# First stage of a two-layer perceiver kernel: queries and values moved between the key chunks, ones rows filled later, maxima over 96 rows

## What is computed

```python
def _L0_xattn_ref(queries, keys, values, Wq, bq, Wk, bk, Wv, bv, Wo, bo):
    q = (queries @ Wq + bq).reshape(B, L, 16, 8).transpose(0, 2, 1, 3)
    k = (keys @ Wk + bk).reshape(B, S, 16, 8).transpose(0, 2, 1, 3)
    v = (values @ Wv + bv).reshape(B, S, 16, 8).transpose(0, 2, 1, 3)
    weights = jax.nn.softmax(jnp.einsum('bhld,bhsd->bhls', q, k) * SCALE, axis=-1)
    out = jnp.einsum('bhls,bhsd->bhld', weights, v).transpose(0, 2, 1, 3).reshape(B, L, 128)
    return out @ Wo + bo

x = x + _L0_xattn_ref(_layernorm(x), ctx, ctx, ...)
x = x + _L0_attn_ref(_layernorm(x), ...)
x = x + _L0_ffn_ref(_layernorm(x), ...)
# and the same three again for layer 1, whose cross attention normalises queries and keys by head
```

## Time and profile before

| | us |
|---|---|
| median of 3 runs (362.95 to 363.93) | 363.71 |
| span of the profiled execution | 361.7 |
| PE busy | 317.0 (88%) |
| DVE busy | 229.4 (63%) |
| ACT busy | 169.4 (47%) |
| POOL busy | 30.6 (8%) |

### The profile page before, as it was taken

The page is one execution under the profiler, slowest core; times in us unless marked ns, Lnnn a source line. Parts: engine busy times, 40 slices in busy tenths (PEclk is TensorE's granted clock), DMA queues, the critical chain, the costliest instruction groups (busy, mean ns, idle before and its releaser), DMA issues.

```text
span 361.7 us, 7735 instructions
## 1 busy us (share of the span) xinstructions
PE 317.0 (88%) x3308; PEld 207.6 (57%) x3308; DVE 229.4 (63%) x452; ACT 169.4 (47%) x224; POOL 30.6 (8%) x22
## 2 busy tenths in 40 slices
PE   3899989899899998998766998989989998556976
PEld 1356757567576763555254665757756675233646
DVE  6687687777777003663986788777777601536753
ACT  2344435455456677694943234545645576012000
POOL 9400000000000003331340000000000000000000
PEclk9999999999999999998989899999999999675999
DMA  7645974453670000101053999853469400000000
GB/s 258 231 98 114 253 156 100 102 114 72 157 327 2 2 4 0 44 10 36 2 106 81 198 353 402 203 116 90 89 162 461 190 2 3 0 2 1 2 0 5
DMA packets 8114, 41.12 MB, mean 114 GB/s; under 512 B 2192, under 2 KB 2512, under 8 KB 7568
## 3 DMA queue, kind: packets, MB, share of 16 engines
q1 hardware_dynamic: 7936, 40.32, 39.4%
q10 hardware_dynamic: 144, 0.31, 0.3%
HBM read 21.32 MB, written 0.03 MB: 59 GB/s over the span
## 4 chain that ended last, share of the span: by engine, by line
PE 75%; DVE 15%; ACT 5%; issue 2%; DMA 1%; POOL 0%; DVEq 0%; ACTq 0%
PE ps L836 74%; DVE mx L512 2%; DVE arena L546 2%; DVE arena L549 2%; DVE y L494 1%; DMA consts<-in_const 1%; ACT arena L381 1%; DVE qst L530 1%; ACT arena L383 1%; ACT prob L403 1%; DVE arena L557 1%; PE ps L853 0%; PE ps L1009 0%; ACT lnv L410 0%; DVE st L490 0%
## 5 line engine op out<-in xcount | busy, mean ns | idle before, releaser
L403 ACT ACTIVATE prob<-ps 128x1024 f32<-128x1024 f32 (+1 forms) x104 | 101.3, 976 | 77.2 <-PE ps L836 77.2
L512 DVE TENSOR_REDUCE mx<-ps 128x1 f32<-128x512 f32 (+1 forms) x156 | 101.5, 660 | 25.0 <-PE ps L836 23.8
L836 PE MATMUL ps<-kst,qst 128*128 128x512 f32 (+1 forms) x208 | 87.6, 447 | 8.2 <-DVE mx L512 4.3
L836 PE MATMUL ps<-qst,kst 128*128 128x256 f32 x392 | 68.1, 293 | 1.0 <-DVE qst L530 1.0
L836 PE MATMUL ps<-prob,vaug 128*18 128x128 f32 x1568 | 65.2, 276 | 0.5 <-ACT prob L403 0.5
L836 PEld LDWEIGHTS ps<-qst,kst 128*128 128x128 f32 x392 | 57.6, 189 | 10.9 <-issue 5.9
L836 PEld LDWEIGHTS ps<-kst,qst 128*128 128x128 f32 x208 | 37.6, 189 | 33.4 <-issue 23.8
L836 PEld LDWEIGHTS ps<-prob,vaug 128*18 128x18 f32 x1568 | 36.5, 97 | 21.8 <-issue 16.5
L518 DVE TENSOR_REDUCE mx<-ps 128x2 f32<-128x1024 f32 (+1 forms) x26 | 29.6, 1160 | 7.3 <-PE ps L836 7.2
L361 ACT ACTIVATE vaug<-ps 128x512 f32<-128x512 f32 (+1 forms) x26 | 14.8, 573 | 28.1 <-PE ps L836 27.7
L537 DVE COPY avsb<-ps 128x256 f32<-128x256 f32 x8 | 3.4, 420 | 33.9 <-PE ps L836 33.9
(11 more groups left out here) (194 smaller groups left out, 273.1 us busy)
## 6 DMA issues: line engine op xcount, KB each, us to landing
kst<-arena SPq DMA_DIRECT2D x48, 192.0 KB, 3.3
kst<-arena SPq DMA_DIRECT2D x48, 128.0 KB, 2.5
arena<-in_experts SPq DMA_DIRECT2D x1, 5760.0 KB, 18.3
kst<-arena SPq DMA_DIRECT2D x24, 144.0 KB, 2.5
w<-in_experts SPq DMA_DIRECT2D x1, 3456.0 KB, 13.0
w<-in_late SPq DMA_DIRECT2D x1, 3284.5 KB, 12.1
arena<-in_experts SPq DMA_DIRECT2D x1, 3072.0 KB, 16.0
arena<-in_ctxT SPq DMA_DIRECT2D x2, 768.0 KB, 8.0
```

The costliest lines, as they stand in the source:

```text
L403: nc.scalar.activation(prob[:, B % 2, 0:w], ps[:, b0:b0 + 2, :].rearrange("p a b -> p (a b)")[:, 0:w], ACT.Exp, scale=XSCALE).then_inc(exp ...
L512: V.reduce_max(mx[:, p, k:k + 1], ps[:, 4 + m % 2, 0:width(k)], AX).then_inc(max_read, 1)
L836: return mm(out_, lhsT, rhs, start=start, stop=stop, skip_group_check=True)
```

## The change

The first stage gets another order, in all three compute engines. On PE it becomes: key chunk 0, the transpose, the queries, value chunk 0, key chunk 1, value chunk 1, key chunk 2, value chunk 2, key chunk 3, value chunk 3, and then a loop over c from 0 to 12 of key chunk c + 4, the maxima of c, and from c = 4 on value chunk c. ACT follows the same order. DVE does split 0, the queries, splits 1 to 3, and in the loop split c + 4 and the reduce of c.

POOL waits for `q_ready` before it fills the ones of `kst`, and fills partitions 96 and 97 alone. The maxima of both layers run over 96 partitions (QROWS) and the scores over 98 (KROWS). The zeros of `qst` in partitions 96 to 127, one memset on DVE at the start and one on POOL between the layers, are dropped, and with them PE's wait for the second.

```diff
-KEYS_AHEAD = 6
+KEYS_AHEAD = 4
 def v_schedule(c):
-    return range(min(NB, max(0, c - 2) + max(0, c - 10)), min(NB, max(0, c - 1) + max(0, c - 9)))
+    return range(c + KEYS_AHEAD, c + KEYS_AHEAD + 1) if c < 0 else range(c, min(NB, c + 1)) if c >= KEYS_AHEAD else range(0)
@@ POOL
             pool.wait_ge(v_ones, 1)
+            pool.wait_ge(q_ready, 1)
             for s in range(2):
-                nc.gpsimd.memset(kst[QROWS:P, s, :].bitcast(F32), 1.0).then_inc(ones_set, 1)
+                nc.gpsimd.memset(kst[QROWS:KROWS, s, :].bitcast(F32), 1.0).then_inc(ones_set, 1)
-            nc.gpsimd.memset(qst[QROWS:P, :, :].bitcast(F32), 0.0).then_inc(ev("shift_zero"), 1)
-            pool.wait_ge(ev("shift_zero"), 1)
@@ DVE
-            V.memset(qst[QROWS:P, :, :].bitcast(F32), 0.0)
             split(0)
-            split(1)
             stack_queries()
-            for c in range(2, KEYS_AHEAD):
+            for c in range(1, KEYS_AHEAD):
                 split(c)
@@ PE
-                return one(ps[:, bnk, 0:width(k)], qst[:, G % NG, p * P:(p + 1) * P], kst[:, G % 2, a:b])
+                return one(ps[:, bnk, 0:width(k)], qst[0:QROWS, G % NG, p * P:(p + 1) * P], kst[0:QROWS, G % 2, a:b])
-                    last = one(dst[:, t * GQ:(t + 1) * GQ], kst[:, G % 2, a:a + P], qst[:, G % NG, :])
+                    last = one(dst[:, t * GQ:(t + 1) * GQ], kst[0:KROWS, G % 2, a:a + P], qst[0:KROWS, G % NG, :])
             yT_of("ln0")
-            key_chunk(0, 1, view["wk0"])
             ...
-            for c in range(2, KEYS_AHEAD):
-                key_chunk(0, c, view["wk0"])
-            for c in range(NB):
-                if c + KEYS_AHEAD < NB:
+            for c in range(-KEYS_AHEAD, NB):
+                if 0 < c + KEYS_AHEAD < NB:
                     key_chunk(0, c + KEYS_AHEAD, view["wk0"])
                 if c == 0:
                     pe.wait_ge(q_ready, 1)
-                    pe.wait_ge(ones_set, 1)
-                max_pair(0, c)
+                if c >= 0:
+                    max_pair(0, c)
                 for v in v_schedule(c):
                     v_chunk(0, v, view["wv0"])
-            pe.wait_ge(ev("shift_zero"), 1)
```

## The result

The changed kernel takes 384.34 us in the median (378.44 to 386.38) against 363.71 before. The ratio is 1.048 (95% interval 1.043 to 1.054), taken of those executions in which the clock of TensorE dropped least; the medians stand at 1.057. The forecast was 368.4, with a range to 371.3. The direction was right and the size four times too small.

The account below looks back on a forecast made before the run. PE was taken to bound the first stage and what follows. -2.4 + 6.9 + 0.9 = +5.4, or +3.8 if the clock rises earlier; +4.7 gave span 366.4, plus 2.0 is 368.4 us, range 365.3 to 371.3.

Parts of the forecast that it names:

- Part 1, the front: Start of the first stage: queries start earlier, maxima 0 comes at about 18.9 us with more values done, 2.4 us ahead.
- early clock: Case in the first stage's front: PE's clock rises one step earlier, 1.6 us more, so 4.0 us ahead.
- Part 2, the stacks: First stage's loop, KEYS_AHEAD 6 to 4: PE stands before maxima 4, 7 and 10 for key copies, 6.9 us.
- The path to the split: First stage: from key chunk 6's start on PE to the end of its split on DVE, 2.64 us.
- The landing: Key copies to `kst`: the last lands 3.3 us after issue for maxima 4, 2.6 us for maxima 10.
- Part 3, group 1's stack: End of the first stage: PE waits for the first key copies of the next group, 0.9 us more.
- the rival of the clock: Behind the stand before maxima 4 the clock falls, 1.7 us of work lost, time 370.1 us; chance 0.15.
- maxima over 96 rows ... I take nothing: Matmuls of both layers: maxima over 96 rows instead of 128 and scores over 98 change nothing, 0 us.
- The edits at nothing: Dropped `qst` memsets, later `kst` memsets and fewer matmul rows, all counted at 0 us.
- 0.87 for slower: Whole kernel: chance 0.87 that the change makes it slower, against 0.07 faster and 0.06 same.
- The middle of +5.4 and +3.8: Whole kernel: sum with the clock rising as before (+5.4) or earlier (+3.8); the middle taken was +4.7 us.

Follow-up runs that it names:

- e1_order: The new order alone on the kernel before, with the memsets and all matmuls over 128 partitions as before: 373.01 us against 362.22.
- g3_again: The changed kernel itself, run again without any edit: 379.15 us and 396.6 us.
- e3_ahead6: The changed kernel with KEYS_AHEAD back at 6 instead of 4: 375.34 us, ratio 1.033 to the kernel before.
- g2_ranges: The finer ranges: e1_order with the key chunk ranges KC cut into eight instead of five: 368.66 us, ratio 1.017 to the kernel before.
- e8_order_busy: e1_order with four idle key projections on PE ahead of the waits of maxima 4 and 10: 368.81 us, ratio 1.018 to the kernel before.

## Why the prediction was wrong, point by point

**Part 1, the front: right.** M0 was forecast at 18.9, or earlier with an early clock, and came at 18.36. The clock's record at the high level begins at 12.5 us instead of 14.5, so a part of the early rise was there. Value chunk 1 took 1.09 us at 12.62, where key chunk 1 before it had taken 1.98. 2.9 us ahead against 2.4.

**Part 2, the stacks: right in mechanism, somewhat small.** 6.9 forecast, 8.5 measured: 4.39 before M4 (3.95 forecast), 0.29 before M7 (1.2; it was 1.03 in e1_order and 1.01 in g3_again), 3.56 before M10 (1.75), and 0.27 before M2. The path to the split was as priced, since the copies for maxima 4 start at 24.04. The landing was not:

```profile
L272 SPq DMA_DIRECT2D kst<-arena x3: 507/592/595, 24.0 to 25.2; - x3
DMA to landing us min/median/max: 2.7/3.2/4.4
```

The last copy lands 4.4 us after its issue where I took 3.3, and that of maxima 10 4.6 where I took 2.6. The finer ranges show that the wait for the range's last chunk is the cause of the stands.

**Part 3, group 1's stack: priced at 0.9, not seen.** By the stands and the slow clock PE was so late that the stack was there (its first matmul at 55.90 waits 0.38 us, for ACT). The wait is real: 3.20 us in e3_ahead6 and 1.99 in g2_ranges.

**The step that failed first: the rival of the clock.** I had it as one possible drop of 1.7 us behind one stand, with a chance of 0.15, and argued that the other stands were short. There were drops behind both, an estimated 5.1 us of lost work in the profiled execution, and 4.4 in e1_order against e8_order_busy. The earlier trace rows showed the low level behind a stretch with 0.62 of 3.41 us busy, I had worked out a stand of 3.95 us myself, and I had no row with a stand of that length and the high level behind it. The drop should have been a term of the sum and not a rival. The rule of the Trainium skill that was cited there, from "TensorE: Matmul & The Clock Gate", told the direction; the trace agrees with it: 0.00 busy from 26.12 to 29.53, then a granted clock of 0.50.

**The step that failed most: "maxima over 96 rows ... I take nothing".** The durations bear it out: a pair of maxima still takes 1.02 to 1.03 us. But the price of an edit to a matmul is not only its duration. Without the order, the rest of the change costs 6.4 us in the median (368.59 - 362.22), a number that hangs on how many of the executions are long, and 2.4 by the ratio of 1.007. With it, the whole change costs 384.34 - 363.71 = 20.6 and the order alone 373.01 - 362.22 = 10.8, which leaves 9.8 us for the rows; by the ratios of 1.048 and 1.030 it is an estimated 6.7. I compared a 96-row group with a 128-row group by its mean time, and did not ask whether it holds the clock the same. The forecast put 0 on it and had no bound for a loss.

**The edits at nothing otherwise: right.** The later memsets delayed nobody: splits beside them take 0.74 to 0.75 us.

**Sign, sum and chances.** 0.87 for slower was borne out. The middle of +5.4 and +3.8 is +4.6 and not +4.7, which changes nothing. The profiled execution lies 10.0 us above the forecast (378.44 - 368.4). 5.1 of it are the drops behind the stands, 3.4 the third drop, 1.6 the longer stands, less the 0.9 of part 3 that didn't come: 9.2. The range had room for one drop of 1.7 us where this trace holds three that cost 8.5, and executions of the kernel then differ by 8 us and more.

## What to carry to other kernels

When an edit opens a stand of some microseconds on TensorE, put the work behind it at the lower clock into the sum, and look at every light stretch that follows, since one drop can last for 17 us. What a look-ahead has to cover is counted from the last chunk of a transfer's range, not from its first: count PE's work from that chunk's projection to the first use of the range. And cutting rows of a matmul can cost time though no matmul gets longer. Here it did so in some executions and not in others, so a few executions would have missed it.

## What the hardware showed that was not expected

Fewer rows and the clock. With 96 and 98 partitions instead of 128 and nothing else changed, the kernel before has two executions at 363 us and two at 375 and 376, with granted clocks of 0.957 and 0.913 to 0.918. With 128 it never took more than 367.67 us in 62 executions. By what way the hardware comes to it is not shown.

The latest copy of a stack. In the stretch from 24 to 30 us of the changed kernel, the DMA queues held one transfer of instructions beside the copies:

```profile
q1 hardware_dynamic: 144, 0.59, 47.4%
q8 instruction: 1, 0.02, 1.0%
```

In the kernel before, the same three copies ran with no such transfer beside them and the last landed 3.3 us after its issue, against 4.4 here. The other traces go the same way: in e1_order and e8_order_busy the copies for maxima 4 have no such transfer beside them and the last lands after 3.3 us, in g3_again they have one and it lands after 4.4. The copies for maxima 10 have one in the changed kernel and in e1_order and land after 4.6 and 4.5, where before had none and 2.6. One case goes against it: before's copies for chunks 7 to 9 had one too and landed after 3.3. That the instruction transfer holds up one of the engines is argued from these pairs and was not tried.

How the drops multiply stays open: the changed kernel ranges from 378 to 397 us over seven executions, and only the two fastest of them were profiled.
